# Edge filters as strip products over gray rows that pass through DRAM

## The chip, the cores and the metric

One core of one Trainium2 chip runs the whole network in one program. The time is the device time of one execution in microseconds; lower is better. It is quoted as the median of the timed runs, and beside it stands one profiled execution, whose trace all rows below are taken from.

## The reference

Eight RGB images of 256x256 become gray images; two 3x3 Scharr filters run over each; half the sum of the two magnitudes is an edge map of 256 rows of 256 values. With 128 text rows it gives 384 tokens of 256 channels per image. Two transformer blocks follow (attention with 16 heads and two kinds of keys, a feed-forward network with four-bit blocks, anchor attention, a mixture of 8 experts). Only the beginning is touched by this change:

```python
w = (0.2989, 0.587, 0.114)
gray = einsum('bchw,c->bhw', x, w)[:, None]           # x: 8, 3, 256, 256
edges = conv(gray, scharr, padding='SAME')            # two 3x3 filters
edge = sqrt(square(edges)).sum(axis=1) / 2            # 8, 256, 256
h = concatenate([edge, txt], axis=1)                  # 8, 384, 256
h = h + attention(layernorm(h), ...)                  # W_Q, W_K, W_K_prime, W_V, W_O
...
```

## The kernel before

Everything that this case speaks of lies in the function `attention0`, in the opening stage: from the start to the first call of `turn`, the attention of image 0. Each engine has its own program, in the order in which it is written, and the programs meet at semaphores.

**Gray and edges.** `image(i)` (L427) loads the three channels of an image into `pix` (two buffers, used in turn). `make_gray(i)` (L1078) makes the gray image on DVE with three instructions. Rows of the image lie on 128 partitions, two halves beside each other, with a zero column at either side. A vertical tap is then a product with a banded 128x128 matrix (`band`, built by DVE from `masks` and `taps`), a horizontal tap a shift by one column. So `edges(i, n)` (L676) has for each of the two filters three products of 128x512 (L688) and one of 6 rows (L692), which adds the rows that are missing where the two halves meet. Those rows are fetched by `sides(i)` (L852), two small transfers from ACT's queue. `magnitudes(i)` (L836) takes absolute values on ACT, `edge_rows(i)` (L1088) adds them into `h` on DVE, `moments(i)` (L1093) takes the moments for the layer norm.

**Preparing an image for attention.** `inputs` normalizes, PE turns it (L550) and projects it (`project`, L559, six pieces, and `project_v`, L567). ACT, DVE and GpSimd (POOL) split each piece of queries and keys into three bfloat16 parts (`high_part`, both `low_parts`). SP stores the parts in DRAM (`store_parts`, L374) and fetches them back by heads (`stacks`, L385, 18 transfers for each half of the heads, each to 16 partitions). `qs` and `ks` are what they fill.

**The ring.** Before image i can be attended to, the maximum of each row of its scores is needed: `ring` does 96 products (L588) into three PSUM banks in turn, and DVE reduces each (L961). SP writes the negated maxima into `qs` (`maxima`, L394), eight transfers for image 0. For image 0 the ring runs by itself, in 33 rounds of 3, and the preparation of image 1 lies in rounds 0 to 7. Its first half needs `stacks(0, 0, 0)`, its second, from round 17 on, `stacks(0, 0, 1)`.

**What sets the order.** PE does the edges of image 0, turns five weights, does the edges of image 1, projects image 0, does the edges of images 2 to 5 in one piece, then the ring, into which it puts the 16 products of images 6 and 7 one a round (`edge_piece`). DVE makes the gray images early, between other work. Every transfer but those of `sides` is issued by SP, so all of them stand in the one queue q1, in the order of SP's program:

```python
for i in range(2, B):
    image(i)
sp.wait_ge(kinds_made.sem, 4)
kinds(0)
store_parts(0)
stacks(0, 0, 0)
stacks(0, 0, 1)
sp.wait_ge(edges_done.sem, edges_done.at(BESIDE, 0))
kinds(1)
```

after which come `store_parts(1)`, `stacks(1, 1, 0)` and the maxima of image 0. `kinds` writes constant rows into four partitions of `ks`.

Of the kernel before, what the change touches and what calls it, by code (L numbers as in the profile page):

```python
# [14 lines left out]
B = 8  # L15
# [152 lines left out]
def attention0(nc, block, G, E, x, txt, scharr, wq, wk, wv, wkp, wo, alpha, wgate, wup, wdown):  # L168
# [5 lines left out]
    OFFS = (-1, 0, 1)  # L174
# [31 lines left out]
    TAPS = [(f, kx) for f in range(2) for kx in range(4)]  # L206
    BESIDE = 6
# [3 lines left out]

    def edge_piece(r):

        j, n = divmod(r - len(PREPARE), len(TAPS))
        return (j + BESIDE, n) if 0 <= j < B - BESIDE else (None, None)

    def edges_before(r, back):

        i, n = edge_piece(r - back)
        return i if n == len(TAPS) - 1 else None  # L220
# [14 lines left out]
    with ExitStack() as ctx:  # L235
# [26 lines left out]
        taps = sb("taps", [P, 2, 3, 3])  # L262
# [15 lines left out]
        band = in_prob(2, 3, P).rearrange("p (f k n) -> p f k n", f=2, k=3)  # L278
        corner = in_prob(2, P)[0:6].rearrange("p (f n) -> p f n", f=2)
        masks = in_prob(len(OFFS), P).rearrange("p (o n) -> p o n", o=len(OFFS))  # L280
# [4 lines left out]
        GW, SW = 2 * (IMG + 2), 2 * IMG  # L285
        grays = [(k1[:, 0:BESIDE * GW], 0), (in_prob(B - BESIDE, GW), BESIDE)]
        side_rows = [(q1[0:6, 0:BESIDE * SW], 0), (in_prob(B - BESIDE, SW)[0:6], BESIDE)]

        def place(areas, i, width):

            area, first = areas[i >= BESIDE]
            return area[:, (i - first) * width:(i - first + 1) * width].rearrange("p (a n) -> p a n", a=2)

        def gray_of(i):
            return place(grays, i, GW)

        def side_of(i):
            return place(side_rows, i, SW)
# [37 lines left out]
        pix_in = [sig(f"pix_in{u}", 48) for u in range(2)]  # L336
        side_in = [sig(f"side_in{i}") for i in range(B)]
        side_zero, corner_in = sig("side_zero"), sig("corner_in")
        masks_done, ident_done, bands_done, borders = sig("masks_done"), sig("ident_done"), sig("bands_done"), sig("borders")
        gray_step, edges_done, mag_done, h_edge = sig("gray_step", 3), sig("edges_done", 1), sig("mag_done", 2), sig("h_edge", 1)  # L340
# [29 lines left out]
        def _(sp):  # L370
# [56 lines left out]
            def image(i):  # L427

                if i >= 2:
                    sp.wait_ge(gray_step.sem, gray_step.at(i - 1, 0))  # L430
                for ch in range(3):
                    sp.dma_start(pix[:, i % 2, ch], x[i, ch].rearrange("(a p) c -> p a c", p=P)
                                 ).then_inc(pix_in[i % 2].sem, 16)
# [2025 lines left out]
```

## Time and profile before

| | us |
|---|---|
| timed runs, median (lowest to highest) of 3 | 1815.2 (1815.18 to 1818.09) |
| profiled execution, device time | 1817.46 |
| its span in the trace | 1815.7 |
| PE busy in it | 1747.6 (96%) |
| first product of the first `turn` | 138.07 after the start |

The span runs from the first to the last instruction in the trace; 1.8 us of the profiled execution lie around it. Busy times can overlap and say nothing of which engine the others wait for. In a timeline one line is a run of like instructions of one engine; an entry in brackets is the idle time before it and what ended it. A table by stretch gives for each engine its busy time and the number of instructions, then the granted clock of TensorE (1.00 is 2.4 GHz, 0.50 is 1.2 GHz), the mean busy share of the 16 DMA engines and what they moved. That share counts overlapping packets twice and can pass 1. Where a list of transfers gives a time, it is the median from issue to landing.

### The profile page before, as it was taken

The numbers are of one execution on the slowest core, as the hardware profiler recorded it, in microseconds if no ns is written. First come the engines' busy times: TensorE is split into PE (matmuls) and PEld (weight loads), VectorE is DVE, ScalarE is ACT, GpSimd is POOL, SyncE is SP. The second block draws the span as 40 slices with busy tenths as digits, with TensorE's granted clock in tenths as the row PEclk, the third lists the DMA queues.
The fourth block names the chain that finished last, engine by engine and source line by source line (L and its number), as shares of the span: only waits on it lengthen the run. The fifth ranks groups of instructions, "written<-read, shape, count | busy, mean of one in ns | idle before, by whom it ended". The sixth has DMA issues, their size and how long they took to land.

```text
span 1815.7 us, 29086 instructions
## 1 busy us (share of the span) xinstructions
PE 1747.6 (96%) x9935; PEld 1115.4 (61%) x9935; DVE 1005.1 (55%) x2073; ACT 677.3 (37%) x1290; POOL 409.7 (23%) x415
## 2 busy tenths in 40 slices
PE   7989999899999998999999999999999999999997
PEld 3324444344444435777755666666767679999997
DVE  6597877778788898888865444443211112222221
ACT  2106656566666686545532322233010111111110
POOL 2101120110201003898722221110211211000000
PEclk9988999999999999999999999999999999999999
DMA  6832632426324402000074000000000003423211
GB/s 190 138 66 41 119 78 43 82 45 114 74 47 87 82 2 74 1 0 0 1 294 110 0 0 0 1 1 1 34 28 20 32 20 111 175 104 107 102 32 34
DMA packets 111955, 112.84 MB, mean 62 GB/s; under 512 B 11455, under 2 KB 104433, under 8 KB 111858
## 3 DMA queue, kind: packets, MB, share of 16 engines
q1 hardware_dynamic: 98610, 83.21, 20.3%
q10 hardware_dynamic: 9600, 18.92, 2.9%
q0 software_dynamic: 3648, 9.46, 1.4%
q8 instruction: 55, 0.90, 0.2%
q14 instruction: 42, 0.34, 0.1%
HBM read 78.51 MB, written 32.93 MB: 61 GB/s over the span
## 4 chain that ended last, share of the span: by engine, by line
PE 88%; DVE 7%; issue 2%; ACT 2%; DMA 0%; DVEq 0%; POOL 0%; ACTq 0%; POOLq 0%
PE ps_e L2218 11%; PE ps_e L2151 9%; PE ps_a L614 8%; PE ps_a L588 7%; PE ps_m L1651 6%; PE ps_a L603 6%; PE ps_e L2227 5%; PE ps_m L1794 5%; PE ps_e L2160 5%; PE ps_m L1722 4%; PE ps_m L1752 4%; PE ps_a L559 4%; PE ps_m L1667 3%; DVE mx L961 3%; PE ps_a L688 2%
## 5 line engine op out<-in xcount | busy, mean ns | idle before, releaser
L961 DVE TENSOR_REDUCE mx<-ps_a 128x1 f32<-128x384 f32 x768 | 379.7, 550 | 52.2 <-PE ps_a L588 50.4
L820 ACT ACTIVATE prob<-ps_a 128x768 f32<-128x768 f32 (+1 forms) x512 | 305.7, 650 | 96.7 <-PE ps_a L603 95.7
L588 PE MATMUL ps_a<-w,qs 96*128 96x384 bf16 x768 | 242.1, 338 | 7.7 <-DVE mx L961 3.8
L603 PE MATMUL ps_a<-qs,w 100*128 100x384 bf16 x768 | 207.1, 331 | 5.5 <-issue 4.0
L2218 PEld LDWEIGHTS ps_e<-xTr,w 128*128 128x128 f32 x1792 | 206.0, 193 | 2.2 <-issue 0.8
L2218 PE MATMUL ps_e<-xTr,w 128*128 128x128 f32 x1792 | 206.3, 276 | 0.6 <-DVE xTr L2394 0.6
L588 PEld LDWEIGHTS ps_a<-w,qs 96*128 96x128 bf16 x768 | 72.9, 98 | 182.2 <-DVE mx L961 103.6
L614 PE MATMUL ps_a<-prob,vp 128*32 128x384 f32 x1536 | 163.3, 498 | 0.0
L2151 PE MATMUL ps_e<-xT_all,w 128*128 x448 | 145.7, 486 | 0.0
L2283 ACT ACTIVATE gel_r<-ps_e 128x512 f32<-128x512 f32 x56 | 33.4, 597 | 280.9 <-PE ps_e L2218 280.9
L1651 PE MATMUL ps_m<-w 128*128 128x352 f32 x384 | 122.3, 462 | 2.2 <-ACT w L1828 1.2
L2151 PEld LDWEIGHTS ps_e<-xT_all,w 128*128 128x128 f32 x448 | 85.0, 190 | 57.8
L603 PEld LDWEIGHTS ps_a<-qs,w 100*128 100x128 bf16 x768 | 71.2, 99 | 68.8 <-ACT prob L820 18.0
L2251 ACT ACTIVATE gel<-ps_e 128x384 f32<-128x384 f32 x64 | 31.4, 491 | 203.7 <-PE ps_e L2151 203.7
L2300 DVE TENSOR_TENSOR hid_e<-gel,ps_e 128x384 f32<-128x384 f32 x64 | 35.5, 555 | 129.7 <-ACT gel L2251 129.1
L2227 PE MATMUL ps_e<-w,hid_r 128*128 128x256 f32 x448 | 101.3, 379 | 0.0
L1605 POOL TENSOR_TENSOR attn<-lg,gsum 128x1024 f32<-128x1024 f32 x24 | 45.6, 1902 | 234.6 <-DVE gsum L1487 234.6
L2405 DVE TENSOR_TENSOR hid_r<-gel_r,ps_e 128x512 f32<-128x512 f32 x56 | 38.5, 688 | 102.1 <-ACT gel_r L2283 102.1
L1651 PEld LDWEIGHTS ps_m<-w 128*128 128x128 f32 x384 | 69.9, 190 | 37.7 <-DVE w L1395 2.2
L1722 PE MATMUL ps_m<-wsT,xT_a 128*128 128x512 f32 x192 | 87.1, 596 | 4.8 <-DVE lg L1478 4.8
L516 POOL TENSOR_TENSOR y<-y 128x192 f32<-128x192 f32 x32 | 21.4, 670 | 310.8 <-DVE y L987 310.8
L2133 POOL DMA_INDIRECT out_dram<-y_e,row_id x28 | 27.6, 986 | 278.5 <-DVE row_id L2411 278.5
(266 smaller groups left out, 2585.1 us busy)
## 6 DMA issues: line engine op xcount, KB each, us to landing
w<-parts_dram SPq DMA_DIRECT2D x192, 96.0 KB, 5.2
w<-in_L_ffn_W_dram ACTq DMA_DIRECT2D x18, 1024.0 KB, 8.3
parts_dram<-w SPq DMA_DIRECT2D x24, 576.0 KB, 3.4
qs<-parts_dram SPq DMA_DIRECT2D x96, 96.0 KB, 4.0
prob<-in_x_dram SPq DMA_DIRECT2D x24, 256.0 KB, 3.6
w<-in_L_ffn_W_dram SPq DMA_DIRECT2D x6, 1024.0 KB, 12.8
grouped_x<-empty_row SPq DMA_DIRECT2D x1, 4352.0 KB, 24.3
grouped_h<-empty_row SPq DMA_DIRECT2D x1, 4240.5 KB, 33.9
```

What stands on the lines that cost most here:

```text
L588: mm = pe.matmul(ps[:, r % 3, 0:T], qs[0:NS, b, u // 2, t * P:(t + 1) * P], ks[0:NS, b, u % 2, u // 2], start=True, stop=True)
L603: mm = pe.matmul(ps[:, scores_at(v, more) + t, 0:T], ks[0:NS + 4, b, kp, hh, t * P:(t + 1) * P], qs[0:NS + 4, b, hh], start=True, stop=True)
L614: mm = pe.matmul(ps[j * SLOT:(j + 1) * SLOT, 7, 0:T], vp[:, b, t, g // 2 * QUAD + j], prob[:, g % 2, j, t], start=(t == 0), stop=(t == TT ...
L820: act.activation(prob[:, g % 2, j, ts.start:ts.stop], ps[:, at + ts.start:at + ts.stop, 0:T], ACT.Exp).then_inc(exp_done.sem, 1)
L961: dve.tensor_reduce(at, ps[:, r % 3, 0:T], AX.X, ALU.max).then_inc(ring_free.sem, 1)
L1651: mm = pe.matmul(ps[:, 2 * (u % 2) + n, 0:HALF0], xT[:, t, k], wguT[:, n, k, s * HALF0:(s + 1) * HALF0], start=(k == 0), stop=(k == KC - 1))
L1722: mm = pe.matmul(ps[:, bank + n], xT1[:, k, t * P:(t + 1) * P], wsT[:, k, n * 512:(n + 1) * 512], start=(k == 0), stop=(k == KC - 1))
L1794: mm = pe.matmul(ps[:, 2 + t % 2, 0:C], attnT[:, a, t * P:(t + 1) * P], gs[:, a], start=(a == 0), stop=(a == PAIRS - 1))
L2151: mm = pe.matmul(ps[:, 2 * (a % 2) + m, 0:T], w12[:, 0, m, k, a * P:(a + 1) * P], xT_of(i)[:, k], start=(k == 0), stop=(k == KC - 1))
L2160: mm = pe.matmul(ps[:, 4 + t, 0:C], hid[:, a, t * P:(t + 1) * P], w3[:, 0, a], start=(a == 0), stop=(a == IT1 - 1))
L2218: mm = pe.matmul(ps[:, 2 * n + m, a * P:(a + 1) * P], w12[:, b, m, k, n * HALF1 + a * P:n * HALF1 + (a + 1) * P], xTr[:, k], start=(k == 0 ...
L2227: mm = pe.matmul(ps[:, 4, 0:C], hid_r[:, a], w3[:, b, a], start=(a == 0), stop=(a == IT1 - 1))
```

## The change

The gray image goes through DRAM. `store_gray(i)` writes it, with its zero columns, into `gray_dram` (258 rows of 258 values, the first and last of zeros). `strips(i)` reads it back in three transfers, one for each horizontal shift kx: 34 rows (32 and a neighbour at either side) on 34 partitions, for 8 strips side by side, 256 values each. The three lie below one another on 102 partitions (`im`). One product with a 102x32 matrix (`band`) then does all nine taps of a filter for one strip, and four such products write to four groups of 32 columns (`tile_position`): 16 products of 256 columns for an image, where there were 6 of 512 columns and 2 of 6 rows by 512. `sides`, `corner` and their memsets go away.

Gray images 0 and 1 are still made by DVE. For 2 to 7 ACT scales each channel in place (`scale_gray`) and POOL adds twice (`sum_gray`). POOL also takes over the sum of the magnitudes (`edge_rows`) of images 2 to 7. The edges of image 0 follow the turned weights; those of images 1 and 2 follow the projections; those of 3 to 7 lie whole in rounds 6, 16, 20, 24 and 28 of the ring. `taps` is now read column by column, three transfers of 34x6 single values. ACT has a first square root at the start, so that its table is loaded there.

```diff
-            for i in range(2, B):
-                image(i)
+            store_gray(0)
+            strips(0)
+            image(1)
...
+            image(2)
+            store_gray(1)
+            image(3)
+            strips(1)
+            store_gray(2)
             sp.wait_ge(kinds_made.sem, 4)
             kinds(0)
+            strips(2)
+            store_gray(3)
             store_parts(0)
             stacks(0, 0, 0)
+            image(4)
+            strips(3)
+            image(5)
             stacks(0, 0, 1)
-            sp.wait_ge(edges_done.sem, edges_done.at(BESIDE, 0))
+            for i in range(4, B):
+                store_gray(i)
+                if i + 2 < B:
+                    image(i + 2)
+                strips(i)
             kinds(1)
```

The new functions, on SP, POOL, PE and ACT:

```diff
+            def store_gray(i):
+                if i < BY_DVE:
+                    sp.wait_ge(gray_step.sem, gray_step.at(i + 1, 0))
+                else:
+                    sp.wait_ge(summed.sem, summed.at(i + 1 - BY_DVE, 0))
+                sp.dma_start(gray_dram[i, 1:IMG + 1].rearrange("(a p) n -> p a n", p=P), grays[:, i]
+                             ).then_inc(gray_out[i % 2].sem, 16)
+            def strips(i):
+                sp.wait_ge(row_out.sem, 32)
+                sp.wait_ge(gray_out[i % 2].sem, gray_out[i % 2].at(i // 2 + 1, 0))
+                if i >= 2:
+                    sp.wait_ge(edges_done.sem, edges_done.at(i - 1, 0))
+                for kx in range(3):
+                    corner = gray_dram[i, 0:1, kx:kx + 1]
+                    rows = bass.AP(corner.tensor, corner.offset, [[PAD, HALO], [STRIP * PAD, STRIPS], [1, IMG]])
+                    sp.dma_start(im[kx * HALO:(kx + 1) * HALO, i % 2], rows).then_inc(im_in[i % 2].sem, 16)
...
+            def sum_gray(i):
+                j, g = i - BY_DVE, gray_of(i)
+                pool.wait_ge(scaled_done.sem, scaled_done.at(j, 2))
+                pool.wait_ge(borders.sem, 2)
+                pool.tensor_tensor(g, pix[:, i % 2, 0], pix[:, i % 2, 1], ALU.add).then_inc(summed.sem, 1)
+                pool.wait_ge(scaled_done.sem, scaled_done.at(j, 3))
+                pool.wait_ge(summed.sem, summed.at(j, 1))
+                pool.tensor_tensor(g, g, pix[:, i % 2, 2], ALU.add).then_inc(summed.sem, 1)
...
+            def edges(i):
+                u = i % 2
+                pe.wait_ge(im_in[u].sem, im_in[u].at(i // 2 + 1, 0))
+                if i >= 2:
+                    pe.wait_ge(mag_done.sem, mag_done.at(i - 1, 0))
+                else:
+                    pe.wait_ge(bands_done.sem, 6)
+                for f in range(2):
+                    for a in range(2):
+                        for c in range(STRIPS // 2):
+                            mm = pe.matmul(ps[c * STRIP:(c + 1) * STRIP, 4 + 2 * u + f, a * IMG:(a + 1) * IMG], band[0:ROWS, f],
+                                           im[0:ROWS, u, a * (STRIPS // 2) + c], start=True, stop=True, tile_position=(0, c * STRIP))
                     mm.then_inc(edges_done.sem, 1)
...
+            def scale_gray(i):
+                u = i % 2
+                act.wait_ge(pix_in[u].sem, pix_in[u].at(i // 2 + 1, 0))
+                for ch in range(3):
+                    act.mul(pix[:, u, ch], pix[:, u, ch], GRAY[ch]).then_inc(scaled_done.sem, 1)
```

**On SP's queue**, between the text rows and the second half of the first stacks, this stood before (each row is a line, what it writes and reads, the rows, pieces and elements of one transfer, and how many):

```order
L443 DMA h<-in_txt_dram 128x8x256
L432 DMA prob<-in_x_dram 128x2x256 x3
L446 DMA al<-in_L_attn_alpha_dram 128x1
L432 DMA prob<-in_x_dram 128x2x256 x18
L450 DMA w<-kind_rows 4x16x384 x2
L374 DMA parts_dram<-w 128x6x384 x3
L385 DMA qs<-parts_dram 16x8x384 x6
L385 DMA w<-parts_dram 16x8x384 x12
```

and this stands there now, from the store of gray image 1 to the load of image 5:

```order
L433 DMA gray_dram<-w 128x2x258
L424 DMA prob<-in_x_dram 128x2x256 x3
L445 DMA prob<-gray_dram 34x8x256 x3
L433 DMA gray_dram<-w 128x2x258
L471 DMA w<-kind_rows 4x16x384 x2
L445 DMA prob<-gray_dram 34x8x256 x3
L433 DMA gray_dram<-w 128x2x258
L364 DMA parts_dram<-w 128x6x384 x3
L375 DMA qs<-parts_dram 16x8x384 x6
L375 DMA w<-parts_dram 16x8x384 x12
L424 DMA prob<-in_x_dram 128x2x256 x3
L445 DMA prob<-gray_dram 34x8x256 x3
```

Stores of gray images and strips (L445) have moved in between the loads, the parts and the stacks; the parts of image 0 (L364, before L374) stand behind three strips.

**On PE**, this stood around the projections (behind L567 the first two rows stand eight more times, for images 2 to 5, and then the ring begins):

```order
L688 MATMUL ps_a<-w,prob 128x512 x3
L692 MATMUL ps_a<-qs,prob 128x512
L550 MATMUL ps_a<-ident,w 128x128 x6
L559 MATMUL ps_a<-w,wT 128x384 x12
L567 MATMUL ps_a<-wT,w 128x256 x6
```

and this stands from there to the middle of the ring now:

```order
L744 MATMUL ps_a<-prob,band 32x256 x16
L607 MATMUL ps_a<-ident,w 128x128 x6
L616 MATMUL ps_a<-w,wT 128x384 x12
L624 MATMUL ps_a<-wT,w 128x256 x6
L744 MATMUL ps_a<-prob,band 32x256 x32
L645 MATMUL ps_a<-w,qs 128x384 x3
```

The edges (L744) of image 0 now stand ahead of its projections (L616) and directly behind the turned weights, and two images instead of four stand between the projections and the ring (L645, before L588).

## Rows read from the trace of the kernel before

**Rows 1.** Table by stretch: stretch and length, busy by engine, clock, DMA share, GB/s.
```profile
core 0: us, PE busy (x) PEld busy (x) DVE busy (x) ACT busy (x) POOL busy (x), PEclk, DMA share, GB/s
0.00:15.00 15.00, 5.11 (x6) 1.85 (x6) 8.70 (x27) 0.00 (x0) 4.91 (x16) 1.00 0.84 269
15.00:76.00 61.00, 59.64 (x152) 26.04 (x152) 32.75 (x73) 15.37 (x29) 9.58 (x12) 0.94 0.77 161
76.00:138.00 62.00, 52.71 (x161) 19.66 (x160) 54.77 (x125) 7.36 (x15) 8.76 (x12) 0.88 0.36 65
```
**Rows 2.** Timeline of PE: start, length, engine, line, operation; projections, edges, ring, first turn.
```profile
33.59 9.70 PE L559 MATMUL ps_a<-w,wT 128*128 128x384 f32 x24 [1.12 <-ACT w L783]
...
72.38 2.84 PE L688 MATMUL ps_a<-w,prob 128*128 128x512 f32 x6
75.15 1.12 PE L692 MATMUL ps_a<-qs,prob 6*128 6x512 f32 x2
...
138.07 0.80 PE L603 MATMUL ps_a<-qs,w 100*128 100x384 bf16 x2
```
**Rows 3.** Timeline of DVE: a gray image, an edge map to its inputs, twelve reductions.
```profile
23.64 0.68 DVE L1091 TENSOR_TENSOR h<-prob 128x512 f32<-128x512 f32 x1
...
27.29 1.06 DVE L939 TENSOR_SCALAR w<-h,mv,rstd 128x256 f32<-128x256 f32 x3
28.26 0.42 DVE L1083 TENSOR_SCALAR w<-prob 128x512 f32<-128x512 f32 x1
28.72 1.42 DVE L1086 SCALAR_TENSOR_TENSOR w<-prob,w 128x512 f32<-128x512 f32 x2
...
97.34 5.81 DVE L961 TENSOR_REDUCE mx<-ps_a 128x1 f32<-128x384 f32 x12
```
**Rows 4.** Timeline of SP's queue: issues of parts, stacks and maxima.
```profile
51.57 3.36 SPq L385 DMA_DIRECT2D qs<-parts_dram  x6
54.97 5.85 SPq L385 DMA_DIRECT2D w<-parts_dram  x12
...
87.96 11.52 SPq L374 DMA_DIRECT2D parts_dram<-w  x3
```
**Rows 5.** Transfers of ACT's queue, 0 to 150: queue, packets, MB; issues, KB each.
```profile
q10 hardware_dynamic: 96, 0.05, 0.1%
...
qs<-w ACTq DMA_DIRECT2D x12, 3.0 KB
...
prob<-prob ACTq DMA_DIRECT2D x4, 3.0 KB
```
**Rows 6.** Transfers from 178 to 184: the four maxima of half an image.
```profile
DMA packets 146, 0.03 MB, mean 4 GB/s; under 512 B 144, under 2 KB 146, under 8 KB 146
...
qs<-mneg SPq DMA_DIRECT2D x4, 6.0 KB
```
**Rows 7.** Table by stretch: loads, stores, stacks, and the two `kinds` alone (78.5 on).
```profile
13.00:13.50 0.50, 0.50 (x2) 0.00 (x0) 0.00 (x0) 0.00 (x0) 0.50 (x2) 1.00 1.08 354
...
88.50:89.00 0.50, 0.37 (x2) 0.10 (x1) 0.50 (x2) 0.00 (x0) 0.00 (x0) 1.00 0.15 54
89.00:89.50 0.50, 0.38 (x2) 0.21 (x2) 0.50 (x2) 0.00 (x0) 0.07 (x1) 1.00 1.09 373
...
64.00:65.00 1.00, 1.00 (x3) 0.27 (x2) 0.16 (x3) 0.00 (x0) 0.00 (x0) 1.00 1.17 142
...
78.50:80.00 1.50, 1.50 (x7) 0.84 (x6) 1.34 (x4) 0.48 (x1) 0.00 (x0) 0.50 0.24 38
80.00:81.50 1.50, 1.50 (x4) 0.89 (x4) 1.20 (x3) 0.00 (x0) 0.00 (x0) 0.50 0.20 24
```
**Rows 8.** Issues of the whole execution: KB each, median us to landing.
```profile
parts_dram<-w SPq DMA_DIRECT2D x24, 576.0 KB, 3.4
...
w<-kind_rows SPq DMA_DIRECT2D x4, 48.0 KB
...
wg<-in_L_ffn_Wg_dram SPq DMA_DIRECT2D x1, 8.0 KB, 1.7
```
**Rows 9.** Costliest groups: busy, mean ns of one; products on 32 columns, POOL's sums.
```profile
L614 PE MATMUL ps_a<-prob,vp 128*32 128x384 f32 x1536 | 163.3, 498 | 0.0
...
L1605 POOL TENSOR_TENSOR attn<-lg,gsum 128x1024 f32<-128x1024 f32 x24 | 45.6, 1902 | 234.6 <-DVE gsum L1487 234.6
```
**Rows 10.** Timeline of ACT: magnitudes of image 0.
```profile
21.91 1.09 ACT L843 ACTIVATE prob<-ps_a 128x512 f32<-128x512 f32 x2 [0.46 <-PE ps_a L692]
```

More of the change, by code:

```diff
@@ L205, in attention0 @@
     FIRST = -(-NR // EARLY)
-    TAPS = [(f, kx) for f in range(2) for kx in range(4)]
-    BESIDE = 6
+    STRIP = 32
+    HALO = STRIP + 2
+    ROWS = 3 * HALO
+    STRIPS = IMG // STRIP
+    PAD = IMG + 2
+    BY_DVE = 2
+    CONV_AT = {6: 3, 16: 4, 20: 5, 24: 6, 28: 7}
     def first_ring(r):
         return range(r * EARLY, min((r + 1) * EARLY, NR))
[L212 to L220, printed above, removed]
     def scores_at(v, more):
@@ L704, in turn_weight @@
                 mm.then_inc(wTd.sem, 1)
-            pe.wait_ge(corner_in.sem, 32)
-            for n in range(len(TAPS)):
-                edges(0, n)
             pe.wait_ge(ident_done.sem, 1)
@@ L712, in _ @@
                 turn_weight(n)
-            for n in range(len(TAPS)):
-                edges(1, n)
+            edges(0)
             pe.wait_ge(wTe.sem, 5)
@@ L723, in _ @@
                 freed.append((signal, n + 1))
-            for i in range(2, BESIDE):
-                for n in range(len(TAPS)):
-                    edges(i, n)
+            edges(1)
+            edges(2)
             pe.wait_ge(rest_done.sem, rest_done.at(0, 3 * KC))
@@ L733, in _ @@
                     last = in_bank3(PREPARE[r][0], 1, PREPARE[r][1], last)
-                i, n = edge_piece(r)
-                if i is not None:
-                    edges(i, n)
+                if r in CONV_AT:
+                    edges(CONV_AT[r])
             for b in range(2):
@@ L850, in roots @@
                 act.activation(rstd[:, tiles], mv[:, tiles, 1], ACT.Sqrt, bias=eps[:]).then_inc(root_done.sem, 1)
-            def sides(i):
-                gray, side = gray_of(i), side_of(i)
-                act.wait_ge(gray_step.sem, gray_step.at(i, 3))
-                act.wait_ge(side_zero.sem, 2 if i < 2 else 4)
-                for a, row in ((1, gray[0:1, 1, 0:IMG]), (0, gray[P - 1:P, 0, 0:IMG])):
-                    shifted = bass.AP(row.tensor, row.offset, [list(row.ap[0]), [1, 3], [1, IMG]])
-                    act.dma_start(side[3 * (1 - a):3 * (2 - a), 1 - a], shifted).then_inc(side_in[i].sem, 16)
-            act.wait_ge(borders.sem, 3)
-            sides(0)
-            sides(1)
-            magnitudes(0)
+            act.wait_ge(borders.sem, 1)
+            act.activation(rstd[:, 0:1], eps[:], ACT.Sqrt, bias=eps[:]).then_inc(root_done.sem, 1)
             for n in range(5):
@@ L1134, in _ @@
[L1134 to L1139 removed]
+                to = band[0:ROWS, f]
+                dve.tensor_scalar(to, masks[0:ROWS, 0], taps[0:ROWS, f, 0:1], None, ALU.mult).then_inc(bands_done.sem, 1)
@@ L1140, in _ @@
+                n += 1
+                for ky in (1, 2):
+                    dve.wait_ge(bands_done.sem, n)
+                    dve.scalar_tensor_tensor(to, masks[0:ROWS, ky], taps[0:ROWS, f, ky:ky + 1], to, ALU.mult, ALU.add
+                                             ).then_inc(bands_done.sem, 1)
+                    n += 1
+            dve.wait_ge(borders.sem, 2)
+            make_gray(0)
             edge_rows(0)
@@ L1164, in _ @@
                     low_parts(1, PREPARE[r][1])
-                if r == 2:
-                    edge_rows(BESIDE - 1)
-                if r == 3:
-                    moments(BESIDE - 1)
-                i = edges_before(r, 2)
-                if i is not None:
-                    edge_rows(i)
-                    moments(i)
+                if r in MOMENTS_AT:
+                    moments(MOMENTS_AT[r])
             inverses(2, 2, B)
```

205 lines of the change are left out of this document (92 added, 113 removed).

## The prediction

> **What bounds the kernel now.** I read the table by stretch first, since the change touches only the opening stage. Up to 15 us the kernel waits for transfers; from 15 to 76 PE is busy 59.6 of 61 us; from 76 to 138 DVE leads with 54.8 of 62 [rows 1]. Then PE's timeline: the projections of image 0 run from 33.6 to 43.3, eight groups of edge products (2.84 + 1.12 us each, not quite end to end) fill PE from 45.7 to 76.2, the ring follows, and the first `turn` begins at 138.07 [rows 2]. Behind that nothing is changed. So the forecast is one number: when the first turn begins. It needs the ring's end, `stacks(1, 1, 0)` and the first maxima. Last, the transfers: before, SP's queue was ready in time everywhere, with a mean DMA share of 0.77 and 0.36 in the two stretches [rows 1].
>
> **PE, DVE, ACT and POOL.** Edges cost PE 2 x 3.8 = 7.6 us an image [rows 2]. The new 16 products go four abreast: 1536 records on 32 columns of 384 take 163.3 us, two records to a product, so four products 0.85 us [rows 9]; for 256 columns 0.57, for an image 2.3. That takes 4 x 7.6 = 30.5 us out from between projections and ring and puts 4.6 in. DVE loses six gray images (1.84 each) and six sums (0.68) [rows 3]. ACT gains 18 scalings at some 0.54, the price of a magnitude of the same 512 values [rows 10]: 9.7 us. POOL gains 18 sums of 512 values; half of the 1.90 for 1024 values [rows 9] is 0.95 each, 17 us. Both have room: ACT is busy 22.7, POOL 18.3 of 123 us [rows 1]. The sums of images 4 to 7 stand behind POOL's low parts of image 1, done by round 8 of the ring. Were strips free, the ring would wait for the stacks and not for PE, and this side would bring a few us (first rival).
>
> **The strips: over how many DMA engines?** One transfer is 34 x 8 pieces of 1 KB, 278.5 KB; an image needs three, 836 KB. ACT's queue shows how a small transfer is spread: 16 transfers of 3 rows of 1 KB make 48 data packets, and 96 are counted, so 3 closing packets to a transfer [rows 5]. Four maxima of 24 rows of 256 B make 96 data packets, and 144 small ones are counted, 12 closing packets to a transfer [rows 6]. The two `kinds`, 4 rows each, run at a share of 0.20 to 0.24, close to 4 of 16 engines [rows 7]. I read a closing packet as one engine. Then 3 rows use 3 engines, 4 use 4, 24 use 12: always equal numbers of rows. For 34 rows, equal numbers on at most 16 engines means 2 engines of 17 rows. No row shows an uneven split, so I take 2; the other reading (at most 3 rows to each, 12 engines) is a rival.
>
> The Trainium skill ("DMA: Bandwidth & Descriptors", section "Why a DMA increments its semaphore by 16 and not by 1") states this: the engines are the largest number up to 16 that divides the slowest dimension of both sides, the lowest-numbered ones, with 100 partitions on 10 engines as an example. By that rule the strips lie on the same two engines always. The rows above agree for 3, 4 and 24; none here shows 34.
>
> **Rate of one engine.** Loads with 1 KB pieces, eight to a row for the text, run at 354 GB/s on 16 engines, 22.1 each; parts stores at 373, 23.3 each [rows 7]. The stacks (one row to an engine) reach 142, 8.9 each, and the kinds 24 to 38 on four, 6 to 9.5 each [rows 7]. A strip engine has 17 rows and 8 KB to a row, and is nearest to the text load. I take 22.1: 278.5 / 44.2 = 6.3 us a transfer, **18.9 us an image**, 151 for eight. The low end is 17.9 (23.3); the kinds' rate is a rival.
>
> **The strips are in the way of everything.** All transfers share one queue, and a transfer over 16 engines is complete when the two slow engines have done their sixteenth. So each later store, load or stack waits on those two for the strips ahead of it, and `strips(i)` waits for its gray image's store, which is such a transfer. A parts store shows the fixed cost: first issued at 87.96 [rows 4], moving only late in 88.5 to 89 [rows 7], so 1.0 us ahead; of its 3.4 us [rows 8] 1.6 are transfer, which leaves some 0.6 at the end. From one image's strips to the next: store 0.75 + 0.6 + 1.0 = **2.4 us**.
>
> **The sum, in us from the start.**
> - The `taps`, 204 pieces of 4 B in each of three transfers, lie on two engines too, 306 pieces on each, ahead of image 0. The nearest row is `wg`, 16 pieces of 32 B an engine in 1.7 us altogether [rows 8]. Bounds: nothing, or 1.7 / 16 = 0.11 each, 32 us. With 1.3 us of fixed cost off, 0.025 each: 7.7 us. Landed at 10, image 0 at 12.2, gray (1.84) at 14.1.
> - On the two engines the five weights (3.6) and the text (2.9) are ahead of the gray store: it lands at 19.6. Strips 0: +1.0 + 18.9 + 0.6 = **40**.
> - Edges, 1.1 for magnitudes [rows 10], sum, moments, root, inputs: from the start of the magnitudes to the end of the inputs it was 6.4 with a table load of 1.3 in it [rows 3, 10]; with the edges some 8.4. Then gray 1: 50.2, since `make_gray(1)` stands behind `inputs(0)` on DVE. Stored at 52.6. Strips 1, with image 3 ahead, 54.2 to 73.1. The projections run meanwhile, from 50.
> - Strips 2: 75.5 to 94.4. Gray 3 and the first part of image 0 land at 97.3; the parts were ready at some 65. Stacks: 9.2 to issue [rows 4], 12.4 to move (1.77 MB at 142 GB/s): **the ring starts at 111**, where it started at 76.2.
> - Image 4, strips 3: 112.9 to 131.8; round 6 of the ring waits for them some 8 us.
> - Image 5 and the second stacks (5 us on the two late engines, at 22.1), gray 4, image 6, strips 4: 144.2 to 163.1. Strips 5: 166 to 184.9. Strips 6: 187.3 to 206.2. Strips 7: 208.5 to 227.4. The ring stands at rounds 16, 20, 24 and 28 for each of them; a round is only 1.5 us of reductions (5.81 for twelve) [rows 3]. It ends at about 236.
> - `store_parts(1)` is now behind strips 7: first part landed at 229.6, 18 stacks issued by 238.8, four maxima by 241.8, landed at 243.5.
> - **First turn at 244 instead of 138: +106.**
>
> From the profiled execution's own 1817.5 (1815.7 of span and 1.8 around it; 0.1% above the median): 1817.5 + 106 = 1923.5. I forecast **1923**.
>
> **Rival 1, uneven split: faster or level.** If 34 rows go to 12 engines, three to each, an image's strips take 3.3 us. Image 0 projects at some 29 (was 33.6), the parts are ready at 45, gray 3 is stored at 48, the stacks land at 66: the ring starts 10 us earlier. But six moments lie in it instead of three and its reductions are the same, some 63 us, and SP's tail (strips 7, parts, stacks, maxima, 18 us) comes to 134: 4 us gained, 1813. The point from which the change pays is where strips and handover fit the four rounds (6 us) from one image to the next: 3.6 us of strips, nine engines or more. For it: no row shows 34. Against it: each shape seen is split evenly.
>
> **Rival 2, few engines are slow each.** At the kinds' 6 to 9.5 GB/s an engine, a transfer takes 15 to 23 us and an image 44 to 70, 200 to 400 us more in all: 2125 to 2325. For it: the only transfer seen on four engines is that slow. Against: it reads and writes just 4 partitions, and the 16-partition stacks are slow in the same way on all 16 engines.
>
> **Rival 3, ACT or POOL late.** Were their steps twice as long, sums would come some 3 us later; store and strips would still be behind the earlier strips. It is worth under 5 us within the forecast's case and moves nothing in rival 1 but the gain: 1817.
>
> **How the numbers follow.** Two engines at the loads' rate: 0.81. Rival 1: 0.13, half of it (with rival 3 on top) within the bound. Rival 2: 0.06. Within the first case: taps free and 17.9 us an image give 1923 - 8 - 8, some 1907, and waits that I put in a row and that overlap up to 15 less; taps at their upper bound +24, strips a tenth slower +15, other waits +20: 1982. Range 1890 to 1985; rivals 1 and 2 are what is left out. A measurement can tell 0.2% (3.6 us) from no change. Faster 0.07, same 0.05, slower 0.88.
>
> **What the profile will show.** If right: long stretches of a DMA share near 0.13 and 40 to 45 GB/s; the third strip transfer lands some 19 us after its issue; 17 rows' worth and two closing packets to a transfer; the ring starts near 111 with PE idle before L645, released by a transfer; PE's waits at L744 are for transfers, about 12 us each from image 4 on, and the clock falls there; the turn begins near 244. If the share is near 0.7 while strips move and the ring starts near 66, rival 1 holds. If the share is 0.13 and the rate under 20 GB/s, rival 2. What would make me wrong besides: strips that begin before the queue's earlier transfers are done, or `taps` that cost tens of us.

## The result and the profile after

The changed kernel takes 1940.5 us (median of 4 runs, 1939.0 to 1941.1) where the kernel before took 1815.5 (1815.2 to 1818.1, 4 runs): a ratio of 1.068 with an interval of 1.0665 to 1.0702. It is 125 us slower. The forecast was 1923, with a range of 1890 to 1985.

| profiled execution | before | after |
|---|---|---|
| span, us | 1815.7 | 1939.1 |
| PE busy, us (share) | 1747.6 (96%) | 1725.2 (89%) |
| DVE / ACT / POOL busy, us | 1005 / 677 / 410 | 981 / 687 / 430 |
| mean granted clock | 0.988 | 0.943 |
| projections of image 0 begin | 33.59 | 53.35 |
| ring begins | 76.20 | 116.53 |
| first turn begins | 138.07 | 262.25 |
| from there to the end of the span | 1677.6 | 1676.9 |

The last row places the loss: all of it lies before the first turn. The page of the kernel after says the same in three lines: the granted clock in 40 slices of 48.5 us each, the engines' shares of the chain that ended last, and the group of the strip products (busy and mean ns, then idle time and its releaser).
```profile
PEclk7665579999999999999999999999999999999999
PE 72%; DVE 10%; DMA 7%; SPq 5%; issue 3%; ACT 3%; POOL 1%; DVEq 0%; ACTq 0%; POOLq 0%
L744 PE MATMUL ps_a<-prob,band 102*32 102x256 f32 x256 | 29.1, 634 | 110.8 <-DMA prob<-gray_dram 110.8
```
The products of all eight images take 29.1 us and PE waits 110.8 us ahead of them, every time for a strip transfer. PE's timeline shows seven of these eight waits (start, length, operation; in brackets the idle time before and what ended it). It is the answer to [rows 2].
```profile
42.99 3.64 PE L744 MATMUL ps_a<-prob,band 102*32 102x256 f32 x32 [23.24 <-DMA prob<-gray_dram]
...
53.35 9.78 PE L616 MATMUL ps_a<-w,wT 128*128 128x384 f32 x24 [0.57 <-ACT w L829]
...
78.04 3.64 PE L744 MATMUL ps_a<-prob,band 102*32 102x256 f32 x32 [12.31 <-DMA prob<-gray_dram]
99.72 3.64 PE L744 MATMUL ps_a<-prob,band 102*32 102x256 f32 x32 [18.04 <-DMA prob<-gray_dram]
116.53 1.12 PE L645 MATMUL ps_a<-w,qs 96*128 96x384 bf16 x3 [13.18 <-DMA w<-parts_dram]
...
140.90 3.64 PE L744 MATMUL ps_a<-prob,band 102*32 102x256 f32 x32 [6.96 <-DMA prob<-gray_dram]
...
178.44 3.64 PE L744 MATMUL ps_a<-prob,band 102*32 102x256 f32 x32 [12.12 <-DMA prob<-gray_dram]
...
222.31 3.64 PE L744 MATMUL ps_a<-prob,band 102*32 102x256 f32 x32 [12.45 <-DMA prob<-gray_dram]
243.61 3.64 PE L744 MATMUL ps_a<-prob,band 102*32 102x256 f32 x32 [12.35 <-DMA prob<-gray_dram]
...
262.25 0.80 PE L660 MATMUL ps_a<-qs,w 100*128 100x384 bf16 x2 [8.10 <-DMA qs<-mneg]
```
From image 4 on the edges come every 21.3 to 22.5 us; the forecast had 21.2 to 21.8. The table by stretch (columns as in [rows 1]) shows what the transfers do while PE waits.
```profile
21.00:28.00 7.00, 0.00 (x0) 0.00 (x0) 0.00 (x0) 0.00 (x0) 0.00 (x0) 0.63 0.13 41
...
86.00:93.00 7.00, 0.00 (x0) 0.00 (x0) 0.03 (x1) 0.00 (x0) 0.00 (x0) 0.50 0.13 45
```
A share of 0.13 is 2 of 16 engines (0.125), at 41 to 45 GB/s, 20.5 to 22.5 each. The transfers of 21 to 28 us say it once more by their packets.
```profile
DMA packets 281, 0.29 MB, mean 41 GB/s; under 512 B 2, under 2 KB 281, under 8 KB 281
```
One strip transfer and the edge of another run in these 7 us, and two small closing packets are among the 281, as [rows 5, 6] led one to expect of two engines. The Trainium skill ("DMA: Bandwidth & Descriptors", section "Why a DMA increments its semaphore by 16 and not by 1") gives the rule: as many engines as the largest number up to 16 that divides the slowest dimension of both sides. The trace agrees for 34 rows with its 0.13.

SP's queue shows what stands behind the strips (start and length of the issue).
```profile
19.06 9.29 SPq L445 DMA_DIRECT2D prob<-gray_dram  x3
...
52.94 0.37 SPq L433 DMA_DIRECT2D gray_dram<-w  x1
...
56.01 9.75 SPq L445 DMA_DIRECT2D prob<-gray_dram  x3
65.80 5.98 SPq L433 DMA_DIRECT2D gray_dram<-w  x1
```
Here is something the forecast did not have: to issue three strip transfers takes SP 9.75 us, and the one store behind them 5.98 more, where a store that is not behind strips takes 0.37. For that time the issuing engine does nothing else. In the median of the first 270 us a gray store lands 12.4 us after its issue and a parts store 8.1, the latter against 3.4 in [rows 8]:
```profile
parts_dram<-w SPq DMA_DIRECT2D x6, 576.0 KB, 8.1
...
gray_dram<-w SPq DMA_DIRECT2D x8, 258.0 KB, 12.4
```

### The profile page after: what moved, and what is told of

Read it like the earlier page. It is cut to its first block, busy times and chain, and to the rows that moved or that the text cites. A ratio compares the mean times of both kernels' runs of the same rounds, so it can differ in the third digit from the quotient of the medians.

```text
span 1939.1 us, 29382 instructions
## 1 busy us (share of the span) xinstructions
PE 1725.2 (89%) x10063; PEld 1108.1 (57%) x10063; DVE 980.7 (51%) x2032; ACT 687.1 (35%) x1308; POOL 430.3 (22%) x440
## 3 DMA queue, kind: packets, MB, share of 16 engines
q1 hardware_dynamic: 107850, 92.02, 20.6%
## 4 chain that ended last, share of the span: by engine, by line
PE 72%; DVE 10%; DMA 7%; SPq 5%; issue 3%; ACT 3%; POOL 1%; DVEq 0%; ACTq 0%; POOLq 0%
PE ps_e L2241 10%; PE ps_e L2174 8%; PE ps_a L671 7%; PE ps_a L645 6%; PE ps_a L660 5%; PE ps_e L2250 5%; PE ps_e L2183 4%; PE ps_m L1817 4%; PE ps_m L1745 4%; PE ps_m L1775 4%; DMA gray_dram<-w 3%; SPq L445 3%; PE ps_a L616 3%; DMA prob<-gray_dram 2%; PE ps_m L1674 2%
## 5 line engine op out<-in xcount | busy, mean ns | idle before, releaser
L645 PE MATMUL ps_a<-w,qs 96*128 96x384 bf16 x768 | 250.8, 350 | 25.0 <-DMA w<-parts_dram 13.2
L660 PE MATMUL ps_a<-qs,w 100*128 100x384 bf16 x768 | 207.6, 331 | 12.7 <-DMA qs<-mneg 8.1
L645 PEld LDWEIGHTS ps_a<-w,qs 96*128 96x128 bf16 x768 | 73.7, 99 | 201.2 <-DVE mx L1005 105.6
L744 PE MATMUL ps_a<-prob,band 102*32 102x256 f32 x256 | 29.1, 634 | 110.8 <-DMA prob<-gray_dram 110.8
L660 PEld LDWEIGHTS ps_a<-qs,w 100*128 100x128 bf16 x768 | 71.3, 99 | 76.3 <-issue 25.1
```

The source lines that it names most:

```text
L645: mm = pe.matmul(ps[:, r % 3, 0:T], qs[0:NS, b, u // 2, t * P:(t + 1) * P], ks[0:NS, b, u % 2, u // 2], start=True, stop=True)
L660: mm = pe.matmul(ps[:, scores_at(v, more) + t, 0:T], ks[0:NS + 4, b, kp, hh, t * P:(t + 1) * P], qs[0:NS + 4, b, hh], start=True, stop=True)
```

## The experiments

The theory: 34 rows lie on two DMA engines, these two set the pace, and everything in SP's queue waits behind them. The rivals: the bytes, the size of the pieces or their unaligned addresses are slow by themselves; SP's issuing is the bound; ACT, POOL or the order of work is. Unless said otherwise a kernel differs from the changed one only by its edit. "First turn" is the start of PE's first scores product (L603 before, L660 after); 1675 to 1680 us follow behind it in every kernel but one. Ratios are to the kernel before, which was timed again beside each set of experiments and took 1815.5 to 1819.6 us; a difference of 2 us between two sets says nothing. Kernels for which no range is given ran once.

### The same strips over 16 engines

```diff
-                    sp.dma_start(im[kx * HALO:(kx + 1) * HALO, i % 2], rows).then_inc(im_in[i % 2].sem, 16)
+                    for first, end in ((0, 32), (32, 34)):
+                        corner = gray_dram[i, first:first + 1, kx:kx + 1]
+                        rows = bass.AP(corner.tensor, corner.offset, [[PAD, end - first], [STRIP * PAD, STRIPS], [1, IMG]])
+                        sp.dma_start(im[kx * HALO + first:kx * HALO + end, i % 2], rows).then_inc(im_in[i % 2].sem, 16)
```


> Each strip transfer of 34 rows is cut into one of 32 rows and one of 2; pieces, bytes and results are the same. Theory (34 rows lie on two DMA engines, 17 each, and all else in the queue waits behind them): 32 rows go to 16 engines, an image's strips take 3 to 6 us instead of 19, the first turn begins near 130 to 145 instead of 262, the time is 1805 to 1825. Rival (the transfers are slow because of their pieces, 1 KB at a row pitch of 1032 bytes and shifted by 4, or because gray values must pass through DRAM and back): the time stays within 15 us of 1940.

1838.5 us (1837.3 to 1839.1), ratio 1.011 (1.009 to 1.013). The same bytes in the same pieces, cut 32 + 2 (and the semaphore for them counted to 96 instead of 48), and 102 of the 125 us are gone: the cause is the spread over engines. The figure itself missed the expectation by 13 us. Its table from 22 to 26 us and its PE timeline:
```profile
22.00:26.00 4.00, 0.00 (x0) 0.00 (x0) 0.00 (x0) 0.00 (x0) 0.00 (x0) 1.00 1.11 205
100.00:158.00 58.00, 44.03 (x199) 12.72 (x199) 41.94 (x110) 11.48 (x22) 17.15 (x15) 0.55 0.76 167
```
```profile
77.80 1.12 PE L646 MATMUL ps_a<-w,qs 96*128 96x384 bf16 x3 [12.71 <-DMA w<-parts_dram]
...
109.47 8.40 PE L646 MATMUL ps_a<-w,qs 96*128 96x384 bf16 x18 [6.61 <-DVE mx L1006]
...
158.43 0.80 PE L661 MATMUL ps_a<-qs,w 100*128 100x384 bf16 x2 [3.57 <-DMA qs<-mneg]
```
205 GB/s instead of 41. SP now issues six strip transfers in 2.08 us and the store behind them in 0.38:
```profile
115.39 2.08 SPq L446 DMA_DIRECT2D prob<-gray_dram  x6
117.52 0.38 SPq L433 DMA_DIRECT2D gray_dram<-w  x1
```
The ring starts almost where it did before (77.80 against 76.2), but it lasts 80.6 us and not 61.9. So some 20 us remain that are not the strips' rate.

### On one engine, and with aligned pieces

The first cuts 34 into 17 + 17, with `((0, 17), (17, 34))` in the loop above.

> The same cut in the middle: two transfers of 17 rows instead of one of 34, again the same pieces and bytes. Theory: 17 rows can be split evenly only over one engine, so an image's strips take 38 us instead of 19 (DMA share near 0.06, some 21 GB/s), 8 x 19 = 150 us more: about 2090. Rival (pieces and layout make them slow, or each transfer is spread unevenly over many engines): 1940, no change.

2079.2 us. The share is 0.07 (1 of 16 is 0.063) and the rate 23 GB/s; the edges of the last images come every 39.2 to 39.6 us instead of 21.3:
```profile
26.00:50.00 24.00, 0.00 (x0) 0.00 (x0) 0.00 (x0) 0.00 (x0) 0.00 (x0) 0.50 0.07 23
```
```profile
342.78 3.64 PE L745 MATMUL ps_a<-prob,band 102*32 102x256 f32 x32 [30.47 <-DMA prob<-gray_dram]
382.35 3.64 PE L745 MATMUL ps_a<-prob,band 102*32 102x256 f32 x32 [30.63 <-DMA prob<-gray_dram]
```
The second lays the rows in DRAM 1280 bytes apart instead of 1032 and reads them without the shift by a column (`PITCH = 320`, offset of column 0 for every `kx`), so the horizontal taps see wrong columns.

> The changed kernel with its two-engine strips, but the gray rows in DRAM have a pitch of 1280 bytes instead of 1032, and all three transfers of an image read without the shift of one value (so two of the three thirds of each strip hold unshifted values). Theory (the strips' time is two engines' rate for 1 KB pieces): 41 to 44 GB/s as before, 1930 to 1942. Rival (rows that start anywhere make the reads slow): strips at 46 GB/s or more, two us an image less or better, 1925 or below.

1937.8 us, 46 to 47 GB/s, the last edges every 21.2 us. The rate is the one that the rival named, the time is not: the first turn begins at 258.08, 4.2 us earlier. Pitch and shift together are worth some 3 to 4 us in all, and they are not the cause.
```profile
80.00:85.00 5.00, 0.00 (x0) 0.00 (x0) 3.26 (x12) 0.51 (x2) 0.00 (x0) 0.50 0.14 47
```

### Strips for two images only

```diff
-                for kx in range(3):
+                for kx in range(3 if i < 2 else 0):
...
-                pe.wait_ge(im_in[u].sem, im_in[u].at(i // 2 + 1, 0))
+                pe.wait_ge(im_in[u].sem, im_in[u].at(1, 0))
```
Images 2 to 7 take the strips that images 0 and 1 left in the buffers.

> The strip transfers of images 2 to 7 are left out, the waits on the gray stores stay; edges of images 2 to 7 use the strips of images 0 and 1. Theory: six times 18.9 = 113 us of two engines' time goes away, and the ring can start at about 90, so the first turn begins near 150 to 165 and the time is 1830 to 1845. Rival (the scaling on ACT and the sums on POOL set the pace of images 4 to 7, the strips only fill the time): 1900 or more.

1843.2 us. Here the time misleads. Behind the first turn this kernel takes 1666.1 us, 11 less than all others, and one group of the last stage says why (the kernel after, then this one):
```profile
L2241 PE MATMUL ps_e<-xTr,w 128*128 128x128 f32 x1792 | 204.7, 275 | 0.6 <-DVE xTr L2417 0.6
```
```profile
L2241 PE MATMUL ps_e<-xTr,w 128*128 128x128 f32 x1728 | 197.4, 275 | 0.6 <-DVE xTr L2417 0.6
```
The features are others, and a loop over expert tiles runs less often; that other experts are chosen is the likely reason and not shown. The first turn is free of that: it begins at 175.14, 87 us earlier than 262.25. By this measure the kernel stands at 1854, 10 above what the theory expected, yet far from the rival.

### The strips issued by ACT

SP's `strips(i)` moved to ACT's queue, between its magnitudes.

> The strips are issued from ACT's queue instead of SP's, at the points of ACT's program where their waits are met; everything else stays. Theory, its part on the queue (stores, stacks and parts stand in line behind strips): gray stores land in 4 to 7 us instead of a median of 12.4, stacks are not held up by a whole image, and the time falls by 5 to 25 us to 1915 to 1935, not more, since the two engines still have 8 x 19 us of strips to move. Rival (the order in the queue does not matter, the engines' time alone does): within 3 us of 1940; and if ACT, stopped for some 9 us at each issue, is missed elsewhere, slower.

1954.4 us: slower, as only the last clause of the expectation allowed. The gray stores did land sooner (5.5 us in the median, not 12.4), but the slow transfers now hold ACT. Its queue:
```profile
97.25 40.45 ACTq L889 DMA_DIRECT2D prob<-gray_dram  x3
```
For 40 us ACT can do nothing but issue these three; parts and magnitudes wait, and the turn begins at 274.27. In this kernel an engine with work of its own is the worse place for a transfer that lies on few engines.

### What keeps the last 20 us

Four kernels on top of the first experiment. The first makes DVE's moments of image 3 in ring round 14 instead of 9, since PE's wait of 6.61 us is for DVE, which waits for that image.
```diff
-            MOMENTS_AT = {2: 2, **{r + 3: i for r, i in CONV_AT.items()}}
+            MOMENTS_AT = {2: 2, 14: 3, **{r + 3: i for r, i in CONV_AT.items() if i > 3}}
```


> On top of the cut 32 + 2: the moments of image 3 move from round 9 to round 14 of the ring. Theory for what is left after the cut (in that kernel DVE stops for some 7 us at its round 9 for POOL's sum of image 3's edges, which stands behind POOL's low parts and the gray sums of images 4 and 5): that stall goes, 4 to 7 us, to 1831 to 1835. Rival (the strips and stores of images 4 to 7 on SP's queue set the ring's pace, the stall is only slack in front of them): within 2 us of 1838.

1838.1 us (1837.0 to 1839.2), nothing gained. The wait went; one for the strips came, and the one for the maxima grew from 3.57 us:
```profile
117.13 3.64 PE L745 MATMUL ps_a<-prob,band 102*32 102x256 f32 x32 [3.11 <-DMA prob<-gray_dram]
...
161.00 0.80 PE L661 MATMUL ps_a<-qs,w 100*128 100x384 bf16 x2 [6.66 <-DMA qs<-mneg]
```
The second also spreads each image's products over four rounds and starts them two rounds earlier (`CONV_AT = {6: 3, 14: 4, 18: 5, 22: 6, 26: 7}`, one quarter a round).

> On top of the cut and the later moments: the 16 edge products of an image in the ring are put as four groups of four into four rounds in a row (images 3 to 7 from rounds 6, 14, 18, 22, 26) instead of all in one. Theory (with only three PSUM banks ahead, DVE runs dry while PE does a whole image's edges, 3.6 us at 1.2 GHz against 1.5 us of reductions, so some 2 us are lost at each of five images): 5 to 10 us below the kernel with only the later moments, 1822 to 1830. Rival (POOL's sums and SP's strips are late for rounds 14 to 26 anyway): no more than 2 us.

1837.2 us (1834.0 to 1839.3), the same, as the rival had it. The third puts parts and stacks ahead of `strips(2)` and `store_gray(3)`, the edges of image 2 into rounds 2 to 5 (with its magnitudes, their sum and its moments later, to match) and the first maxima ahead of the last strips.

> On top of the quarters: parts and stacks of image 0 are issued ahead of the strips of image 2, whose edges move into rounds 2 to 5, and the first half of the maxima is issued ahead of the last strips. Theory (the ring waits 12.7 us for stacks that stand behind a strip, a gray store and their waits, and the first turn waits 3.6 us for maxima behind 18 stacks): ring start 5 to 9 us earlier, the turn's wait gone, 1808 to 1820. Rival (the parts of image 0 are themselves ready late, or POOL's later sum of image 2 pushes the rest): within 3 us of the kernel with the quarters.

1830.8 us (1829.9 to 1832.9), ratio 1.009: 6.5 us gained, where 1808 to 1820 was expected. The ring starts at 72.50, earlier than the 76.20 before the change, and waits inside for the strips of image 4, whose gray store SP issues only at 99.38:
```profile
72.50 1.12 PE L647 MATMUL ps_a<-w,qs 96*128 96x384 bf16 x3 [20.51 <-DMA w<-parts_dram]
...
110.77 1.08 PE L746 MATMUL ps_a<-prob,band 102*32 102x256 f32 x8 [6.76 <-DMA prob<-gray_dram]
```
The fourth makes the gray values of images 4 and 5 during the preparation of image 1 and starts their edges in rounds 11 and 15.

> The reordered kernel (strip transfers in 32 + 2 rows, edges in quarters; 1830.8 us, ring start 72.5, first turn 148.1) with the gray values of images 4 and 5 scaled and summed already in the preparation rounds, the edges one quarter from rounds 2, 6, 11, 15, 19 and 23, and the first maxima between the parts and the stacks of image 1. Theory (the 6.8 us wait in the ring for the gray store of image 4 and the 5.4 us wait before the first turn are late steps of the order, and can be removed): 1812 to 1822 us, first turn 136 to 142 us. Rival (TensorE runs the ring at the lower of its two clocks because it has less work there than before, and its rounds of 2.1 us are the bound): 1827 to 1833 us whatever waits go.

1830.4 us (1830.1 to 1831.1), the rival's time. But the wait that this kernel was to remove is still there, with 5.63 us of the 6.76:
```profile
111.62 1.08 PE L745 MATMUL ps_a<-prob,band 102*32 102x256 f32 x8 [5.63 <-DMA prob<-gray_dram]
```
So it does not settle by itself what the waits cost. What it does show is the stretch behind them: from 120 to 140 us PE has no idle time at all and is still late, at half clock.
```profile
98.00:150.00 52.00, 42.01 (x202) 9.56 (x201) 38.25 (x103) 8.78 (x16) 15.65 (x13) 0.51 0.75 174
...
120.00:140.00 20.00, 20.00 (x109) 4.69 (x109) 16.47 (x42) 3.56 (x7) 5.90 (x5) 0.50 0.70 181
```
A round takes PE 2.09 us here (a quarter of edges 1.08 and three ring products 1.14, overlapping a little). Before, a round was 1.5 us of DVE's reductions [rows 3], at a clock of 0.88 [rows 1].

### TensorE kept busy

The kernel just described, with products added whose result nobody reads:
```diff
+            def idle_products(count):
+                for _ in range(count):
+                    pe.matmul(ps[:, 3], ident[:], wT[:, 0].rearrange("p k c -> p (k c)"), start=True, stop=True)
```
PE also waits, ahead of round 9, for the parts of image 1.

> The early-sums kernel (1830.4 us, first turn 153.6) with work added that nobody reads: TensorE multiplies a turned weight by the identity into an unused bank (128x512 float32, the form that costs 0.46 us in the kernel before and about 0.9 at the lower clock), 20 times in the 20 us in which it waits for the stacks before the ring, 5 times ahead of ring rounds 9 and 11 each, and 10 times ahead of the wait for the strips of image 4 in round 11. Nothing else differs. Theory (what holds the ring back is the lower clock, 0.50 from 98 to 150 us, and TensorE got it because it stood idle in the three waits ahead of it): the granted clock stays at 0.9 or more from 74 to 140 us, the rounds take 1.6 to 1.75 us instead of 2.08, the first turn comes at 140 to 147, 1816 to 1824 us, although work was added. Rival (the clock has nothing to do with those waits, or the strips' arrival paces the rounds): the clock falls to 0.50 all the same, the added products cost up to 5 us, 1829 to 1836 us.

1835.2 us (1833.4 to 1836.8): 5 us slower, the rival's time. But the clock says more than the time. The added products, then the rounds behind them, in PE's timeline:
```profile
97.54 4.56 PE L737 MATMUL ps_a<-wT,ident 128*128 128x512 f32 x10 [0.83 <-DVE w L1008]
...
108.80 8.75 PE L737 MATMUL ps_a<-wT,ident 128*128 128x512 f32 x20
117.47 0.64 PE L752 MATMUL ps_a<-prob,band 102*32 102x256 f32 x8
...
124.36 1.08 PE L752 MATMUL ps_a<-prob,band 102*32 102x256 f32 x8
125.38 1.14 PE L646 MATMUL ps_a<-w,qs 96*128 96x384 bf16 x3
```
```profile
98.00:123.00 25.00, 23.95 (x98) 9.52 (x97) 11.00 (x31) 3.88 (x8) 8.40 (x8) 1.00 0.67 164
123.00:158.00 35.00, 32.93 (x149) 7.62 (x150) 30.60 (x79) 5.37 (x10) 7.47 (x6) 0.50 0.78 161
```
With the products the clock stays at 1.00 from 98 to 123 us, where it was 0.51 from 98 to 150 without them, and a quarter costs 0.64 us instead of 1.08; the four rounds behind the products begin 1.2 to 1.6 us apart and not 2.09. Behind the last of them the clock falls, though PE is busy 32.9 of 35 us with strip and ring products. So the theory is half right: the clock changes with what PE does and sets the length of the rounds, but idle time is not all that brings it down. My products were also mis-sized: one is two records, 0.91 us and not 0.46, so that the edges of image 4 began at 117.47, where they began at 111.62 without them. What the ring would take at the full clock without added work was not reached by any run. Of the 20 us behind the cut the new order won 6.5; no run took away the rest, and how it divides between the clock, the waits for strips and the gray half stays open.

### The gray half alone, and image 5 in the ring of the kernel before

The kernel before with only its gray values of images 2 to 7 made by ACT and POOL; edges, taps and borders as before.
```diff
                else:
+                    scale_gray(i)
+                    act.wait_ge(summed.sem, summed.at(i + 1 - BY_DVE, 0))
```


> The kernel before with one half of the change alone: the gray values of images 2 to 7 are scaled on ScalarE (three activations) and summed on GpSimd (two additions); edges, taps, borders and the ring are those of the kernel before, no strips and nothing through DRAM. Theory (the whole loss is the strips' transfers and what they do to the order; the gray half costs nothing by itself): before, VectorE makes the six images in about 3.3 us each beside its other work; ScalarE and GpSimd have slack before the ring, which starts when TensorE ends the edges of image 5 (76.2 us). 1812 to 1821 us, ring start within 76 to 82 us, first turn 136 to 146 us. Rival (the half costs as well: ScalarE does three passes of 0.6 to 0.7 us and two side transfers an image between the magnitudes and the copies, GpSimd 2.4 us an image between the low parts of the weight products): low parts and gray values of images 5 to 7 come late, the ring starts at 85 or later, 1824 to 1832 us; then some of the 20 us that stayed in the spread kernel (1838.5) belong to this half.

1830.4 us (1826.8 to 1834.0), ratio 1.006: 13 us slower, the rival's time, with the ring at 91.64 and the first turn at 155.36. ACT's timeline shows the price of that wait:
```profile
44.54 0.49 ACT L814 ACTIVATE w<-ps_a 128x384 bf16<-128x384 f32 x1 [3.61 <-PE ps_a L579]
44.93 1.66 ACT L880 ACTIVATE prob<-prob 128x512 f32<-128x512 f32 x3
48.77 1.38 ACTq L894 DMA_DIRECT2D qs<-w  x2
50.19 0.49 ACT L814 ACTIVATE w<-ps_a 128x384 bf16<-128x384 f32 x1 [3.61 <-issue]
```
The high parts (L814) come 5.65 us apart here, since between them ACT scales, waits for POOL's sum and issues the borders. In the changed kernel SP stores the gray values and ACT has no such wait, so this cost belongs to the experiment's arrangement. It shows that the half is not free wherever a queue waits for POOL; what it costs inside the change stays open.

Last, what [rows 2] invite: PE's edges of image 5 moved into the ring of the kernel before (images 5 to 7 in rounds 8 to 31), so that the ring waits for the stacks and not for PE.
```diff
+    SPLIT = 5
...
-        return (j + BESIDE, n) if 0 <= j < B - BESIDE else (None, None)
+        return (j + SPLIT, n) if 0 <= j < B - SPLIT else (None, None)
```


> The kernel before with the edges of image 5 also moved into the ring: images 5, 6 and 7, one matrix product a round in rounds 8 to 31 instead of images 6 and 7 in rounds 8 to 23. The ring can then start when the stacks have landed (about 67 to 69 us) instead of at 76.2, and TensorE has less to do before it. Theory (start of the ring bounds the first turn): about 6 us gained, first turn 131 to 134 us, 1807 to 1812 us. Rival (the ring's rounds are bound by VectorE's maxima and by TensorE at its clock there, each edge product put into a round lengthens it): the gain is given back, 1813 to 1817 us, first turn 136 to 140.

1812.9 us (1811.7 to 1815.3, 7 runs), ratio 0.9976 (0.9964 to 0.9989): the fastest kernel of the study, 0.24% below the one before, which took 1817.3 in this set. The time lies 1 us above the expected range, the gain is 4.4 us and not 6.
```profile
68.34 0.66 PE L589 MATMUL ps_a<-w,qs 96*128 96x384 bf16 x3
...
131.81 0.48 PE L604 MATMUL ps_a<-qs,w 100*128 100x384 bf16 x2 [0.28 <-issue]
```
The ring starts 7.9 us earlier and the turn 6.3, as expected. The span gains 5.3: at 136.86 PE waits 3.06 us for ACT inside the turn.

## Why the prediction came out as it did

**Two engines for 34 rows: right.** Share 0.13, two closing packets; 17 rows give 0.07, 32 rows give 1.11. The even splits of [rows 5 to 7] told it, and the uneven split (rival 1) is out.

**22.1 GB/s an engine: right.** 41 to 45 GB/s were measured for two and 23 for one. With nothing large beside them, strips took 20.5 and 20.6 us from issue to edges (images 7 and 6), and 1.0 + 18.9 + 0.6 = 20.5 was the forecast. Rival 2 (6 to 9.5 each) is out: the kinds' low rate in [rows 7] was not that of few engines as such.

**The chain of strips: right in shape, short by 18 us.** Where the strips of each image let PE go, and the first turn:

| | strips 0 | 1 | 2 | ring | 3 | 4 | 5 | 6 | 7 | turn |
|---|---|---|---|---|---|---|---|---|---|---|
| forecast | 40 | 73.1 | 94.4 | 111 | 131.8 | 163.1 | 184.9 | 206.2 | 227.4 | 244 |
| measured | 43.0 | 78.0 | 99.7 | 116.5 | 140.9 | 178.4 | 200.9 | 222.3 | 243.6 | 262.25 |

The differences grow at five places, by 3.0, 1.9, 3.8, 6.2 and 2.0 us.
- Strips 0, +3.0. Taps were used from 9.22 (forecast 10) and the gray image was made at 13.8 (14.1), so this lies in the strips themselves: 23.9 us pass from their issue at 19.06 to the edges, where it is 20.5 for the last two images. In their last 8 us the loads of images 1 and 2 move beside them (first line below; strips alone have a share of 0.13).
- Strips 1, +1.9. Edges cost 3.64 us, not 2.3: the price from [rows 9] was one of the upper clock level (at which they take 1.93, as in the run with 32 + 2 rows), and PE had stood idle for 23 us and had 1.2 GHz. Yet this cost nothing here: from the edges of image 0 to the gray store of image 1, 42.99 to 52.94, 9.95 us pass where 10.2 were forecast. The 1.9 lie behind it: 3.1 us from that store to the strips' issue, forecast 2.4, and 22.0 from there to the edges, forecast 20.5.
- Strips 3, +3.8. The ring's start adds only 0.2 (116.5 for 111). From there to the strips' end the forecast had 20.8 us, image 4's load of 1.9 and 18.9; it took 24.4. Here too large transfers move beside the strips at their end, the load of image 5 and the second stacks (second line).
```profile
30.00:40.00 10.00, 0.00 (x0) 0.00 (x0) 0.00 (x0) 0.00 (x0) 0.00 (x0) 0.50 0.53 130
...
130.00:140.00 10.00, 3.25 (x11) 1.35 (x9) 3.49 (x8) 0.98 (x2) 4.02 (x6) 0.94 0.73 164
```
  The forecast gave the two engines 22.1 GB/s each whatever the other fourteen do. These two strips of eight had the most moving beside them and took the longest; that this slowed them is a guess which no run tested.
- Strips 4, +6.2, the largest. I said that POOL's sums of image 4 stand behind the low parts of image 1, and left that wait out of the sum. The last low part needs the projection of round 7, and PE makes it only behind image 3's edges in round 6, that is, behind strips 3. POOL's timeline:
```profile
148.30 0.50 POOL L537 CAST w<-w 128x384 bf16<-128x384 f32 x1 [11.56 <-DVE w L994]
...
149.75 1.26 POOL L566 TENSOR_TENSOR w<-prob 128x512 f32<-128x512 f32 x1
```
  The sums end at 152.3, and strips 4 were issued at 155.55, where I had them moving at 144.2. A sum costs 1.2 us and not 0.95 (half of one of 1024 values was too little), which is 0.5 of it.
- The tail, +2.0. Up to the first maximum's issue (254.96) it kept its time. From there to the turn 7.3 us pass, where the forecast had 5.2; PE's wait for the maxima is 8.10 us.

**Rival 1's price: wrong.** Had 34 rows been spread, I gave 1813; the run that spreads them takes 1838.5. Two steps of it failed. The ring was to start at 66 and started at 77.80: 9.5 of these 12 us were lost before the projections (38.48, where I had 29), and from the issue of the strips of image 0 (19.00) to its edges (28.12) alone 9.1 us passed, though 3.3 us of transfer were in the price. And the ring lasted 80.6 us instead of some 68, since PE's and DVE's prices were carried over from a kernel in which PE hardly rests: with strips PE has gaps and gets 1.2 GHz (0.55 from 100 to 158 us). Fast transfers alone did not make the change pay.

**Rival 3** did not come as it was put: a scaling on ACT took 0.55 us as priced, a sum on POOL a quarter more and not twice as long. But POOL was late all the same, through PE's order, and SP stood 5.8 us for its sums ahead of the gray store of image 4; that is most of the 6.2 us at strips 4. The forecast's sentence that store and strips would still be behind the earlier strips did not hold there.

## What to carry to other kernels

Before a transfer is written, divide its number of rows by 16: 34 rows used two DMA engines and 32 + 2 rows sixteen, with 102 us between them, and everything behind the slow one in its queue paid too, the issuing engine included. When a change takes work from TensorE and leaves it waiting, price the rest at the lower clock; here a strip product cost 1.9 times as much (3.64 us an image for 1.93) and rounds that another engine used to bound became TensorE's own. A kernel that computes other values can run a different number of tiles later, so compare it at a point ahead of that.

## What the hardware showed that I had not expected

- Behind transfers that lie on two engines, issuing itself became slow: 5.98 us for one store that otherwise takes 0.37, 9.75 us for three strip transfers where six spread ones took 2.08, and 40.45 us for three on ACT. That the queue was full of their pieces is the likely reason; no run shows it.
- TensorE was granted 1.2 GHz in a stretch in which it was busy 32.9 of 35 us with products of 32 output columns and of 96 rows in bf16, and 2.4 GHz over 25 us in which full-size float32 products ran among them. In these two stretches the busy share was nearly the same, 94 and 96%.
- Two engines with 1 KB pieces carried 41 to 45 GB/s, the strips spread over sixteen 205: 20.5 to 22.5 against 12.8 each, at a share of 1.11. Sixteen engines as such are not the reason, since a load over 128 rows, also in 1 KB pieces, ran at 354 [rows 7]; no run says what is.
